# W_o of a macaron block: one load and 32 transposes on TensorE, or two loads, a split on GpSimd and four DMA transposes

## The reference

```python
x = x + 0.5 * ffn(layernorm(x))    # 12 experts of width 32, top 2 by a softmax gate, capacity 107
x = x + attention(layernorm(x))    # 16 heads of 128, causal over the 512 positions of a sequence
x = x + 0.5 * ffn(layernorm(x))    # the same weights again
```

```python
latents = x @ W_down.T; keys = latents @ W_uk.T; values = latents @ W_uv.T
q = x @ W_q.T
ctx = softmax(mask(q @ keys.T / sqrt(128))) @ values      # by head
return ctx @ W_o.T                                        # W_o is 256 x 2048
```

## Time and profile before

| what | value |
|---|---|
| median of 3 runs | 266.6 us (266.31 to 267.62) |
| span of the profiled execution, first to last instruction | 264.7 us |
| PE, DVE, ACT, POOL busy | 247.8, 214.8, 176.1, 70.5 us |
| mean granted TensorE clock | 0.994 of full speed |
| HBM read | 7.55 MB |

### The profile page before, as it was taken

The page is one execution under the profiler, slowest core; times in us unless marked ns, Lnnn a source line. Parts: engine busy times, 40 slices in busy tenths (PEclk is TensorE's granted clock), DMA queues, the critical chain, the costliest instruction groups (busy, mean ns, idle before and its releaser), DMA issues.

```text
span 264.7 us, 7738 instructions
## 1 busy us (share of the span) xinstructions
PE 247.8 (94%) x2755; PEld 189.5 (72%) x2778; DVE 214.8 (81%) x507; ACT 176.1 (67%) x330; POOL 70.5 (27%) x124
## 2 busy tenths in 40 slices
PE   6899897999799999999999999999988999999996
PEld 2754366966668878788886887878876999854355
DVE  2877689996879989999899999999995444578783
ACT  2646770394878979888788897888884333445750
POOL 5130144000004443444343552534550000300310
PEclk9799999999999999999999999999999999999999
DMA  6999000001103011030110302102000000000004
GB/s 228 247 299 357 14 4 0 0 2 40 42 0 74 11 40 40 0 79 0 40 40 10 69 0 49 30 21 59 0 2 2 0 0 2 2 0 1 0 4 159
DMA packets 17832, 13.02 MB, mean 49 GB/s; under 512 B 8524, under 2 KB 17560, under 8 KB 17560
## 3 DMA queue, kind: packets, MB, share of 16 engines
q1 hardware_dynamic: 16616, 11.62, 17.2%
q10 hardware_dynamic: 1200, 1.18, 1.3%
HBM read 7.55 MB, written 1.05 MB: 32 GB/s over the span
## 4 chain that ended last, share of the span: by engine, by line
PE 69%; DVE 19%; ACT 4%; issue 3%; DMA 2%; POOL 1%; ACTq 0%; DVEq 0%
PE bank L847 17%; PE bank L1062 12%; PE bank L875 7%; PE bank L1053 7%; PE bank L1052 4%; PE bank L1076 3%; PE bank L970 3%; PE bank L1075 3%; PE bank L1138 3%; PE bank L1077 3%; PE bank L1009 3%; DVE pT_lo L732 2%; PE bank L1054 2%; DMA w1n<-in_L_ffn_w_dram 2%; DVE nmax L727 2%
## 5 line engine op out<-in xcount | busy, mean ns | idle before, releaser
L469 ACT ACTIVATE prob<-bank,nmax 128x384 f32<-128x384 f32 (+3 forms) x128 | 62.2, 527 | 8.2 <-DVE nmax L723 6.8
L732 DVE TENSOR_TENSOR pT_lo<-bank,pT_hi 128x512 f16<-128x512 f32 x80 | 54.5, 682 | 3.1 <-ACT pT_hi L475 2.4
L475 ACT CAST pT_hi<-bank 128x512 f16<-128x512 f32 x80 | 46.7, 584 | 11.1 <-PE bank L1062 10.6
L1062 PE MATMUL bank<-ident,prob 128*128 128x128 f32 x320 | 50.5, 280 | 0.6 <-ACT prob L469 0.6
L357 POOL TENSOR_TENSOR cst<-craw,rsum 128x256 f32<-128x256 f32 x30 | 18.4, 612 | 94.6 <-DVE craw L741 94.6
L1075 PE MATMUL bank<-lat,pT_hi 128*128 128x65 bf16 x320 | 37.7, 193 | 1.6 <-DVE pT_lo L732 1.6
L1076 PE MATMUL bank<-lat,pT_hi 128*128 128x64 bf16 x320 | 37.8, 195 | 0.0
L1053 PE MATMUL bank<-latT_lo,wqo 128*128 128x384 bf16 (+3 forms) x128 | 36.6, 299 | 1.2
L1077 PE MATMUL bank<-lat,pT_lo 128*128 128x65 bf16 x320 | 37.4, 192 | 0.0
L1075 PEld LDWEIGHTS bank<-lat,pT_hi 128*128 128x128 f16 x320 | 30.1, 96 | 6.5 <-issue 1.4
L1062 PEld LDWEIGHTS bank<-ident,prob 128*128 128x128 f32 x320 | 33.6, 140 | 0.8 <-issue 0.8
(11 more groups left out here) (183 smaller groups left out, 509.6 us busy)
## 6 DMA issues: line engine op xcount, KB each, us to landing
wqo<-stage SPq DMA_DIRECT2D x64, 64.0 KB, 2.0
wqo<-in_L_attn_W_q_dram SPq DMA_DIRECT2D x1, 2048.0 KB, 9.7
wqo<-in_L_attn_W_o_dram SPq DMA_DIRECT2D x1, 2048.0 KB, 14.5
out_dram<-X SPq DMA_DIRECT2D x8, 128.0 KB, 1.8
X<-in_L_attn_x_dram ACTq DMA_DIRECT2D x1, 512.0 KB, 7.0
wuk<-in_L_attn_W_uk_dram SPq DMA_DIRECT2D x1, 512.0 KB, 10.7
wuv<-in_L_attn_W_uv_dram SPq DMA_DIRECT2D x1, 512.0 KB, 9.7
w3n<-in_L_ffn_w_dram SPq DMA_DIRECT2D x1, 384.0 KB, 5.4
```

The source lines that it names most:

```text
L469: last = nc.scalar.activation(prob[:, u % 2, cols], bank[SCORE_BANK[u]][:, cols], ACT.Exp, bias=nmax[:, u, n:n + 1])
L475: nc.scalar.copy(pT_hi[:, j % 2, :], bank[3 + j % 2][:, :]).then_inc(pThi_ready, 1)
L732: nc.vector.tensor_tensor(pT_lo[:, j % 2, :], bank[3 + j % 2][:, :], pT_hi[:, j % 2, :], ALU.subtract).then_inc(pTlo_ready, 1)
L1062: last = nc.tensor.transpose(bank[3 + j % 2][:, blk(k)], prob[:, j % 2, blk(k)], ident[:, :])
```

## The change

W_o gets two more SBUF tensors, `wo_hl`, for its two bf16 parts as it lies. SP loads W_o in two chunks of 128 rows (1 MB each), ahead of W_q, W_uk and W_uv. In POOL's program of `ffn(0)`, behind the gate's steps and ahead of the first L342, stand a copy to bf16 and a subtraction for each chunk, each of 128 x 2048. SP waits for the four results in turn and issues a DMA transpose for each, from `wo_hl` into `woT`, in place of its wait for `woT_hi`. PE's transposes of W_o, ACT's and DVE's `split_woT` and their semaphores are gone. PE waits for all four DMA transposes ahead of Nv.

```diff
+        wo_hl = [sb("wo_hi", [P, DC, H * P], BF16), sb("wo_lo", [P, DC, H * P], BF16)]
...
             sp.dma_start(wdn[:, :], W_down).then_inc(ld["wd"], 16)
+            for c in range(DC):
+                sp.dma_start(wo[:, c, :], W_o[blk(c), :]).then_inc(ld[f"wo{c}"], 16)
             sp.dma_start(wq, W_q.rearrange("(h p) d -> p h d", p=P)).then_inc(ld["wq"], 16)
             sp.dma_start(wuk[:, :, :], W_uk.rearrange("(h p) l -> p h l", p=P)).then_inc(ld["wuk"], 16)
-            sp.dma_start(wo, W_o.rearrange("(c p) n -> p c n", p=P)).then_inc(ld["wo"], 16)
             sp.dma_start(wuv[:, :, :], W_uv.rearrange("(h p) l -> p h l", p=P)).then_inc(ld["wuv"], 16)
-            sp.wait_ge(woT_hi, 8)
+            for c in range(DC):
+                for part, parts_ready in enumerate((wo_hi, wo_lo)):
+                    sp.wait_ge(parts_ready, c + 1)
+                    sp.dma_start_transpose(woT[part][:, :, blk(c)], wo_hl[part][:, c, :]).then_inc(woT_ready, 16)
...
                     nc.gpsimd.tensor_tensor(gate_parts[:, :, 2, :], gate_rest[:, :, :], gate_parts[:, :, 1, :], ALU.subtract).then_inc(gate_step, 1)
+                    for c in range(DC):
+                        pool.wait_ge(ld[f"wo{c}"], 16)
+                        nc.gpsimd.tensor_copy(wo_hl[0][:, c, :], wo[:, c, :]).then_inc(wo_hi, 1)
+                        pool.wait_ge(wo_hi, c + 1)
+                        nc.gpsimd.tensor_tensor(wo_hl[1][:, c, :], wo[:, c, :], wo_hl[0][:, c, :], ALU.subtract).then_inc(wo_lo, 1)
...
-            for k in range(3):
-                split_woT(k)
             split_queries(0, 0)
-            for k in range(3, 8):
-                split_woT(k)
...
-            for k in range(3):
-                transpose_W_o(k)
             pe.wait_ge(m_lo, 4)
             pe.wait_ge(xTlo_ready[1], DC)
             queries(0, 0)
-            for k in range(3, 8):
-                transpose_W_o(k)
...
             pe.wait_ge(wuv_lo, 1)
+            pe.wait_ge(woT_ready, 16 * 2 * DC)
             for k in range(4):
-                pe.wait_ge(woT_lo, (2, 7, 8, 8)[k])
```

More of the change, by code:

```diff
@@ L169, in bass_macaron_moe_mla_moe @@
         bank = [ctx.enter_context(nc.psum_tensor(f"bank{i}", [P, 512], F32)) for i in range(8)]
-        ld = {n: sem(f"ld_{n}") for n in ("x0", "x1", "gate", "w1", "w3", "w2", "wd", "wq", "wuk", "wuv", "wo")}
+        ld = {n: sem(f"ld_{n}") for n in ("x0", "x1", "gate", "w1", "w3", "w2", "wd", "wq", "wuk", "wuv", "wo0", "wo1")}
         consts = sem("consts")
@@ L208, in bass_macaron_moe_mla_moe @@
         m_lo = sem("m_lo")
-        woT_ps = sem("woT_ps")
-        woT_hi = sem("woT_hi")
-        woT_lo = sem("woT_lo")
+        wo_hi = sem("wo_hi")
+        wo_lo = sem("wo_lo")
+        woT_ready = sem("woT_ready")
         wuv_hi = sem("wuv_hi")
@@ L446, in _ @@
                 nc.scalar.copy(xT_hi[:, c, tokens(t)], bank[k][:, :]).then_inc(xThi_ready[1], 1)
-            def split_woT(k):
-                act.wait_ge(woT_ps, k + 1)
-                nc.scalar.copy(woT[0][:, 2 * k:2 * k + 2, :].rearrange("p h d -> p (h d)"), bank[4 + k % 3][:, :]).then_inc(woT_hi, 1)
             def split_N(k):
@@ L700, in _ @@
                                         ALU.subtract).then_inc(xTlo_ready[1], 1)
[L702 to L705, removed]
             def split_N(k):
@@ L1013, in _ @@
                 transpose_xn(1, t, DC * t)
[L1014 to L1025, removed]
             def queries(i, t):
```

## The result

The changed kernel takes 269.92 us (median of 4 runs, 269.64 to 270.57). The kernel before, with a fourth run, takes 266.48. The ratio is 1.0131, with a 95% interval of 1.0102 to 1.0159: it is slower by 1.3%, and the forecast was 269.6. The profiled execution of the changed kernel took 270.57 us, the longest of the four; its span is 268.7 us, 4.0 above the span of the profiled execution before. Two of the ten runs of one experiment, the one with fills, were in a slower state of the chip, and its median and ratio leave them out.

A forecast was written before the change was run, and what follows sets the result against it. The prediction took PE (69% of the chain) and DVE (19%) to bound the kernel. Its terms, -3.8 + 6.1 + 0.7 = +3.0 us, took the median from 266.6 to 269.6 us, range 266.5 to 274.0.

The forecast's parts named there:

- Part 1: W_o's stretch, 52 to 66 us: without PE's transposes the latents follow the first queries directly; -3.8 us.
- Part 2: Loads: W_o's chunks come first, landing at 15.5 and 18.5 us; the loads pushed back cost 0.
- Part 3: Expert choice, 21.45 to 27.99 us: POOL's four operations shut out DVE's operations with two SBUF inputs; +6.1 us.
- Part 4: PE behind the expert choice: the longer idle gap drops its granted clock to half, slowing later work; +0.7 us.
- Part 5: Four DMA transposes of W_o: a few us each, hidden ahead of Nv, where each may take 12.3 us; cost 0.
- the prediction's other estimate: DMA transposes of W_o: 2.0 us for each 512 KB, from the Trainium skill's 261 GB/s.
- sharing: Rival at the expert choice: DVE's small operations run on beside POOL, only slower; 262.8 to 266.3 us, chance 0.14.
- late transposes: Rival ahead of Nv: DMA transposes of 21.6 us each make Nv wait 37 us; 306.8 us, chance 0.04.
- the gain that doesn't arrive: Rival at 56 to 66 us: DVE or the queries' move becomes the link, the loss stays; 273.4 us, chance 0.02.

The follow-up runs named there:

- the one with fills: The changed kernel with four memsets of 128 x 2048 replacing POOL's copies and subtractions, begun when the gate's logits are ready; 264.89 us, ratio 0.991.
- the run of its own: The kernel before with only the load order changed, W_o loaded first in two chunks; 266.25 us, ratio 0.9995.
- POOL's work alone: The kernel before plus early W_o chunks and POOL's four operations, results unused, PE still turning W_o, no DMA transposes; 273.33 us, ratio 1.0243.
- the run with the clock kept up: The changed kernel with 22 further matmuls of constants on PE between hidden(3)'s first part and its wait for the expert choice; 268.46 us.

## Why the prediction was right

The forecast of 269.6 us came out at 269.92, by the mechanism that it named. Step by step:

- *Part 1, the gain.* Forecast 3.8; it measured 4.0 in the profiles of the changed kernel and of the kernel without POOL's work. The latents follow the queries without a gap (3.7, as forecast), and 0.2 lies ahead of the queries (forecast up to 0.3). The queries' move does enter the chain, with `71.68 3.34 DMA wqo<-stage` ahead of scores of the first heads, and PE waits 1.46 us for it there in place of 0.68. But the queries that follow begin 3.70 us late (79.20, before 75.50), as the latents do, so this costs nothing in the end.
- *Part 2, loads.* Forecast 0; 0.05% by the run of its own, inside its interval. The chunks land 5.4 and 7.5 us after issue, at 14.4 and 17.1, a little earlier than placed.
- *Part 3, shutting out.* Forecast 6.1. It measured 6.0 where the timelines met as drawn (POOL's work alone) and 5.0 in the profiled execution of the changed kernel, where chosen slipped by. The net durations, 1.8 and 4.0 us, read from two rows that had waited for each other, were right: 1.9 to 2.0 and 4.1 by the rows. That POOL's reading shuts out DVE's operations with two SBUF inputs is shown by the fills. One thing was misread: L565 has one SBUF input and a constant, so it was no case of this rule but of the second way, which the prediction did not have. It left cp and den out, and that cost nothing only because POOL was done (27.93) when they came (28.66 and 31.16).
- *Part 4, the clock.* Forecast 0.7, measured 1.5 (by the chain, and by the run with the clock kept up), and 0.9 in POOL's work alone. The direction was right and the size was not: the step took 3.3 us of half clock from the earlier trace rows and weighed it against the room until the turning of the gate weights, but the half clock lasted from 29.9 to 36.7, beyond that point, and slowed the work behind it too.
- *Part 5, DMA transposes.* Forecast "a few us each", hidden: 4.5 to 7.6 us to landing, which the prediction's other estimate, 2.0 us, falls short of, and PE never waits. Not foreseen was that SP itself was held: it was busy with the issue of W_uv's load until 22.82, so the first transpose was issued 5 us after its part was ready. With 28 us to spare this costs nothing.

That the sum was nearer than its terms is partly luck: +0.8 on the clock and -0.1 to -1.1 on the shutting out offset each other, and the profiled execution has 1.07 us of another cause at its start and 0.4 at its end. Of the rivals, sharing is refuted by the operations that end just behind POOL's; late transposes by PE's timeline; the gain that doesn't arrive by the latents.

## What to carry to other kernels

An engine with idle time is not free if its operations can shut out those of an engine on the chain, as POOL's do with DVE's here: lay the new work beside the timeline of that engine, operation by operation, and look for the ones with two SBUF inputs and for `tensor_scalar`. The same work cost 6.5 us in one place and let the change gain 1.9% in another; only the waits ahead of it and the order of the transposes differ. And an operation that looks slow in a profile may be standing still: compare its end with the end of what ran on the other engine.

## What the runs showed that was not expected

The layernorm's output operation (`tensor_scalar` with two scalars from memory, 0.41 us for 256 elements) is shut out by POOL's subtractions and copy, four of them stretched from 1.38 to 7.62 us.

One kernel's executions differ by where an early half clock falls. In the profiled execution before it lies from 7 to 11 us, over transposes. In that of the changed kernel it lies later:

```profile
12.00:13.00 1.00, 1.00 (x7) 0.62 (x7) 0.97 (x3) 0.88 (x3) 1.00 (x2) 0.88 1.00 401
13.00:14.00 1.00, 1.00 (x4) 0.33 (x3) 1.00 (x3) 0.45 (x2) 0.18 (x1) 0.50 0.90 361
...
16.00:17.00 1.00, 1.00 (x5) 0.43 (x4) 0.06 (x1) 0.00 (x1) 1.00 (x1) 0.91 0.92 340
```

That is over the first hidden products, behind 1.55 us in which PE stood idle (until 11.22), and eq starts 1.07 us later than before. In the run of POOL's work alone there is none between 5 and 17 us, and eq starts at 20.78. The 46 runs of the kernel before beside the experiments bear this out: 26 of them, with a mean granted clock of 0.999 or 1.000, took 266.0 to 266.5 us, and 20, with 0.993 or 0.994, took 266.9 to 268.2. So the lower clock goes with the longer time; no run was made to test it as the cause.
